# The delta rule's triangular inverses: substitution on VectorE in place of levels on TensorE

## The reference, cut to what matters

```python
def _delta_scan(q_c, k_c, v_c, kb_c, w_c):          # called for each of the two gates
    strict_lower = jnp.tril(jnp.ones((c, c), bool), -1)
    T0 = jnp.where(strict_lower, -(kb_c @ jnp.swapaxes(k_c, -1, -2)), 0.0)
    def inv_body(T, i):                              # row by row: T becomes the inverse, less I
        row = T[..., i, :]
        new = row + jnp.einsum('...k,...kc->...c', row, T)
        new = jnp.where(idx < i, new, row)
        return (T.at[..., i, :].set(new), None)
    T, _ = jax.lax.scan(inv_body, T0, jnp.arange(1, c))
    T = T + jnp.eye(c, dtype=T.dtype)
    u = T @ v_c                                      # kb_c = k * beta, v_c = v * beta
    wm = T @ kb_c
    def step(S, xs):                                 # then a scan over the 8 chunks
        q_i, k_i, u_i, w_i, wm_i = xs
        u_i = (u_i - wm_i @ S) * w_i[..., None]
        a = jnp.where(causal, q_i @ jnp.swapaxes(k_i, -1, -2), 0.0)
        return (S + jnp.swapaxes(k_i, -1, -2) @ u_i, q_i @ S + a @ u_i)
```

## Time and profile before

| | |
|---|---|
| median of 3 runs | 1379.96 us |
| span of the profiled execution | 1391.4 us, 11.4 us over that median |
| PE busy | 1265.5 us (91%), 18034 matmul records |
| DVE busy | 947.4 us (68%), 2038 instructions |
| ACT busy | 738.6 us (53%) |
| POOL busy | 679.6 us (49%) |

### The profile page before, as it was taken

How to read it: one execution, slowest core, us unless ns; L and a number is a source line. 1 busy time by engine, 2 the same in 40 slices (tenths; PEclk the granted TensorE clock), 3 DMA queues, 4 the chain that set the end, 5 groups by cost and what they waited for, 6 DMA issues and landing times.

```text
span 1391.4 us, 43177 instructions
## 1 busy us (share of the span) xinstructions
PE 1265.5 (91%) x18034; PEld 1007.5 (72%) x18034; DVE 947.4 (68%) x2038; ACT 738.6 (53%) x2084; POOL 679.6 (49%) x677
## 2 busy tenths in 40 slices
PE   5776869999999999899999899989999999889898
PEld 3444557777678788678887688767787778778776
DVE  3667688966777876677688668775758775475434
ACT  5577857654745663446765366435774355133221
POOL 3545346763473556256565355443736545304422
PEclk8899899999999999899999999999999999999999
DMA  5101056744366367265676357635565644647662
GB/s 198 59 11 62 1 196 191 228 123 149 114 206 210 128 196 247 95 203 181 215 229 192 104 191 231 206 134 172 168 200 166 206 167 160 221 147 233 189 226 99
DMA packets 90721, 231.44 MB, mean 166 GB/s; under 512 B 9376, under 2 KB 15648, under 8 KB 90400
## 3 DMA queue, kind: packets, MB, share of 16 engines
q1 hardware_dynamic: 90384, 228.09, 50.9%
q10 hardware_dynamic: 144, 0.59, 0.1%
HBM read 225.50 MB, written 3.15 MB: 164 GB/s over the span
## 4 chain that ended last, share of the span: by engine, by line
PE 71%; DVE 12%; issue 4%; ACT 3%; DMA 2%; POOL 1%; DVEq 0%; SPq 0%; ACTq 0%
PE bank L968 15%; PE bank L921 15%; PE bank L831 8%; PE bank L958 4%; PE bank L939 4%; PE bank L616 4%; PE bank L949 2%; PE bank L932 2%; PE bank L687 2%; PE bank L675 2%; DVE ogate L1405 2%; PE bank L711 2%; PE bank L651 1%; PE bank L721 1%; PE bank L661 1%
## 5 line engine op out<-in xcount | busy, mean ns | idle before, releaser
L1802 POOL TENSOR_TENSOR vgate<-vgate,xT 128x512 f32<-128x512 f32 x256 | 323.5, 1288 | 137.8 <-DMA vgate<-gates 137.6
L921 PE MATMUL bank<-wv,vgate 128*128 128x128 f32 x2048 | 258.7, 281 | 5.4 <-POOL vgate L1802 4.7
L921 PEld LDWEIGHTS bank<-wv,vgate 128*128 128x128 f32 x2048 | 247.3, 195 | 16.1 <-issue 11.0
L968 PE MATMUL bank<-ogate,wo 128*128 128x256 f32 x1024 | 251.4, 390 | 3.9 <-DVE ogate L1405 2.7
L968 PEld LDWEIGHTS bank<-ogate,wo 128*128 128x128 f32 x1024 | 191.7, 194 | 35.4 <-issue 10.2
L1405 DVE TENSOR_TENSOR ogate<-ogate,bank 128x1024 f32<-128x1024 f32 x128 | 153.4, 1211 | 37.1 <-PE bank L958 35.6
L1746 POOL TENSOR_TENSOR rot<-rot 128x512 f32<-128x512 f32 x64 | 81.9, 1280 | 108.4 <-DVE rot L1071 108.4
L1516 ACT ACTIVATE prob<-prob,mx 128x128 f32<-128x128 f32 (+1 forms) x256 | 96.0, 377 | 55.9 <-DVE mx L1095 55.6
L1758 POOL TENSOR_TENSOR prob<-prob,rsum 128x256 f32<-128x256 f32 (+1 forms) x64 | 60.1, 939 | 113.9 <-DVE rsum L1098 113.9
L1695 ACT ACTIVATE mprob<-bank,mmin 128x256 f32<-128x256 f32 x128 | 59.3, 469 | 100.7 <-DVE mmin L1394 100.4
L616 PE MATMUL bank<-wqkv,hT 128*128 128x512 f32 x192 | 103.9, 640 | 5.4 <-ACT hT L1452 4.7
(11 more groups left out here) (236 smaller groups left out, 2574.9 us busy)
## 6 DMA issues: line engine op xcount, KB each, us to landing
vgate<-gates SPq DMA_DIRECT2D x128, 512.0 KB, 4.5
ogate<-gates SPq DMA_DIRECT2D x128, 512.0 KB, 4.2
wv<-in_wv_moe SPq DMA_DIRECT2D x128, 256.0 KB, 4.9
wo<-in_wo_moe SPq DMA_DIRECT2D x128, 256.0 KB, 4.7
kv<-values SPq DMA_DIRECT2D x128, 128.0 KB
local<-in_local SPq DMA_DIRECT2D x1, 1715.0 KB, 10.5
wqkv<-in_wqkv SPq DMA_DIRECT2D x2, 768.0 KB, 7.0
x<-in_x SPq DMA_DIRECT2D x8, 128.0 KB, 8.5
```

The lines of the kernel that those rows point to most:

```text
L921: i = nc.tensor.matmul(out[:, n * D:(n + 1) * D], xg[:, e, n * P:(n + 1) * P], m.wv[slot][:, e, :], start=(q, n, e) == (0, 0, 0), stop=(q, ...
L968: i = nc.tensor.matmul(out[:, 0:T], m.wo[slot][:, e, :], cg[:, e, :], start=(h, q, e) == (0, 0, 0), stop=(h, q, e) == (MH - 1, 1, EQ - 1))
L1802: i = tt(gate[:, e:e + half, :], gate[:, e:e + half, :], spread(m.xT[b % 2][:, :], 1, half), ALU.mult)
```

## The change

The 64 systems of an image are solved by substitution on DVE instead of by levels on PE. POOL writes `lower`, the 16 unit lower triangles of each head, times beta, from `kmat` masked to the other side of the diagonal; `w0` has two instructions instead of four. `lanes`: one DVE transpose lays out each system on a partition of its own (4 heads x 2 x 16 systems = 128 partitions: each system twice, once for the even and once for the odd rows of the answer), in 32 rows of 32 columns, and a product with the constant `spot` makes the start of `solved` from beta. `sub`: for k = 31 down to 1, column k of the 16 rows, as far as they are not zero, times row k of the triangle is taken from the columns below k: a product into `step` and a subtraction in place, each of them reading two SBUF tensors. That is 62 instructions an image, each waiting for the one before it, in 8 parts of at most 4 values of k; other DVE work can stand between the parts. `dT` transposes `solved` into `winvT`. The four levels' `lev`, `levmul`, `levmask`, `levadd`, their transposes, `kT`, and ACT's `beta_col` are gone. All turn strings and the bank string are drawn anew, and `wo` on DVE has a wait more.

```diff
+SUBS = [range(k, max(k - 4, 0), -1) for k in range(CH - 1, 0, -4)]
 TENSOR_TURNS = (
-    "aaaaaaaaabbabaXGGGGbabbbaaabaabGaaabbbbbGcaabcbGbbbccbbGcGaabbabGaacaaacGGGbaGcbacbbcaaabbbGaabbGaaabbabbGbcab"
+    "GaaaaGGGaaaabbabXaabbbbabbabbGabacaaGaacabGcbacabGcGbbbaaabbGbaabbaaabbbGGGGcbacacbcGbbbcbbGbabaGbacaaGGcaaabc"
...
 def delta_ticks(b):
-    ticks = [[("kk", b)], [("dstart", b)], [("w0", b)], [], [], [], []]
-    for i in range(1, 5):
-        ticks += [[("lev", b, i)], [("levmask", b, i)], [("levmul", b, i, 0)], [("levmul", b, i, 1)], [("levadd", b, i)]]
-    ticks += [[("dT", b)], [], [], [("uw", b, 0)], [("uw", b, 1)], [("st0", b)]]
+    ticks = [[("kk", b)], [("dstart", b)], [("w0", b)], [("lanes", b)]] + [[("sub", b, part)] for part in range(len(SUBS))]
+    ticks += [[("dT", b)], [("uw", b, 0)], [("uw", b, 1)], [("st0", b)]]
...
-    def lev(b, i):
-        bank = banks.kept("masked", b, i)
-        out = split(take(bank)[:, 0:NC_ * CH], n=NC_)
-        pe.wait_ge(s.winvT, nth_winvT(b, i))
-        w4 = upper_columns(m.winv[:, :, :], i)
-        for c in range(NC_):
-            last = per_head(out[:, c, :].rearrange("p (a n t) -> p a n t", a=2, t=2 ** i), m.kT[:, c, :], w4[:, c::NC_, :, :], start=True, stop=True)
-        last.then_inc(bank.filled, 1)
-
-    def levmul(b, i, a):
...
-        for g in range(a * NC_, (a + 1) * NC_):
-            last = per_head(out[:, g, :], m.winvT[:, g, :], m.pmat[:, g, :], start=True, stop=True)
...
     def wo(b, l):
...
+        before = earlier(b, l, 1)
+        if before:
+            read = banks.of("w2", *before)
+            v.wait_ge(read.emptied, read.use)
...
-    def w0(b):
-        bank = banks.of("kk", b)
-        v.wait_ge(bank.emptied, bank.use)
-        v.chain(nc.vector.transpose(m.kT[:, :, :], m.kmat[:, :, :]))
-
-    def lev(b, i):
...
-        nc.vector.transpose(m.winvT[:, :, :], m.winv[:, :, :]).then_inc(s.winvT, 1)
-
-    def levmask(b, i):
...
-    def levadd(b, i):
...
+    def lanes(b):
+        v.wait_ge(s.w0, nth("w0", b))
+        v.chain(nc.vector.transpose(m.lanes[:, :, :], spread(m.lower[:, :, :], 2, 2)))
+        v.settle()
+        tt(m.solved[:, :, :], m.spot[:, :, :], spread(flat(m.lanes)[:, ::CH + 1], 1, CH // 2), ALU.mult).then_inc(s.lanes, 1)
+
+    def sub(b, part):
+
+        if part == 0:
+            v.wait_ge(s.lanes, nth("lanes", b))
+        for k in SUBS[part]:
+            rows = CH // 2 - k // 2
+            left, step = m.solved[:, k // 2:, 0:k], m.step[:, 0:rows * k].rearrange("p (j c) -> p j c", c=k)
+            v.settle()
+            v.chain(tt(step, spread(m.solved[:, k // 2:, k], 2, k), spread(m.lanes[:, k, 0:k], 1, rows), ALU.mult))
+            v.settle()
+            i = tt(left, left, step, ALU.subtract)
+            if k == 1:
+                i.then_inc(s.sub, 1)
+            else:
+                v.chain(i)
 
     def dT(b):
-        before = banks.kept("level", b, 4)
-        v.wait_ge(before.emptied, before.use)
-        nc.vector.transpose(m.winvT[:, :, :], m.winv[:, :, :]).then_inc(s.winvT, 1)
+        v.wait_ge(s.sub, nth("dT", b))
+        nc.vector.transpose(m.winvT[:, :, :].rearrange("p g i -> p i g"), flat(m.solved)).then_inc(s.winvT, 1)
...
-    def dgate(b, k):
...
-        act(m.beta_col[:, :, :], split(bank.ap, n=NG), ACT.Exp, scale=-1.0).then_inc(bank.emptied, 1)
...
-        a.chain(act(m.beta_col[:, :, :], m.beta_col[:, :, :], ACT.Ln, bias=one))
...
     def w0(b):
...
-        g.chain(tt(m.kmat2[:, :, :], m.kmat[:, :, :], spread(m.level_neg[:, 0:CH], 1, NC_), ALU.mult))
+        g.chain(tt(m.kmat2[:, :, :], m.kmat[:, :, :], spread(m.eye[:, :], 1, NC_), ALU.add))
         g.settle()
...
+        tt(m.lower.rearrange("p t (a c) -> p a c t", a=2), spread(m.kmat2[:, :, :], 1, 2), spread(m.gates[b % 2][:, 0:2, :], 3, CH),
+           ALU.mult).then_inc(s.w0, 1)
```

More of the change, by code:

```diff
@@ L54, in constants @@
     out["eye"] = r == c
-    out["below"] = c < r
+    out["above"] = c > r
     out["upper"] = c >= r
-    level = lambda s, c: (r // (2 * s) == c // (2 * s)) & (r // s % 2 == 1) & (c // s % 2 == 0)
-    upper = lambda s: c[:, c[0] // s % 2 == 0]
-    out["level_neg"] = -1.0 * np.concatenate([level(1, c)] + [level(s, upper(s)) for s in (2, 4, 8, 16)], axis=1)
+    spot = 2 * np.arange(CH // 2)[:, None] + np.arange(2)[:, None, None] == np.arange(CH)[None, :]
+    out["spot"] = np.repeat(spot, NG, axis=0)[np.arange(P) % (2 * NG)]
     out["first"] = np.broadcast_to(ME - np.arange(ME)[None, :], (P, ME))
@@ L158 @@
     "layer1": {"w_delta": (P, 3, D), "conv": (P, 3, CONV), "w_gate": (P, 4, P), "gate_b": (P, 2), "dnorm": (P, CH), "wo_delta": (P, D),
-               "headsum": (P, P), "eye": (P, CH), "below": (P, CH), "upper": (P, CH), "level_neg": (P, CH + 4 * CH // 2), "first": (P, ME),
+               "headsum": (P, P), "eye": (P, CH), "above": (P, CH), "upper": (P, CH), "spot": (P, CH // 2, CH), "first": (P, ME),
                "route": (P, 1), "sel": (P, P)},
@@ L329 @@
 KEPT = [("gla_sum", "gsum", (0,)), ("delta_sum", "dout", (0,)), ("moe_sum", "mproj", (0, 0)), ("values", "hv", (0,)),
-        ("scores", "mscore", ()), ("context", "mctx", ()), ("masked", "lev", ()), ("level", "levmul", (0,))]
+        ("scores", "mscore", ()), ("context", "mctx", ())]
 BANKS = {"xnT": 1, "proj": 1, "projv": 1, "qkT": 1, "lscore": 2, "probT": 1, "pv": 1, "wo": 1, "lnorm": 1,
@@ L334 @@
          "gsend": 1, "fuse": 2, "mqk": 1, "mpT": 1, "mend": 1}
-ON_TENSOR = [*BANKS, "gsum", "dout", "mproj", "hv", "mscore", "mctx", "lev", "levmul", "dwo"]
+ON_TENSOR = [*BANKS, "gsum", "dout", "mproj", "hv", "mscore", "mctx", "dwo"]
 class Banks:
@@ L864, in uw @@
         pe.wait_ge(s.vkc, nth("dstart", b))
[L865 removed]
+        pe.wait_ge(s.winvT, nth("dT", b))
         for c in range(NC_):
@@ L1300, in kk @@
         out = filled(bank).rearrange("p (c a t) -> p c a t", c=NC_, a=2)
-        v.chain(tt(m.kmat[:, :, :], out[:, :, 1, :], spread(m.below[:, :], 1, NC_), ALU.mult))
+        v.chain(tt(m.kmat[:, :, :], out[:, :, 1, :], spread(m.above[:, :], 1, NC_), ALU.mult))
         tt(m.do[:, :, :], out[:, :, 0, :], spread(m.upper[:, :], 1, NC_), ALU.mult).then_inc(bank.emptied, 1)
-    def w0(b):
-        bank = banks.of("kk", b)
-        v.wait_ge(bank.emptied, bank.use)
-        v.chain(nc.vector.transpose(m.kT[:, :, :], m.kmat[:, :, :]))
@@ L1324, in levadd @@
-    def levadd(b, i):
-        bank = banks.kept("level", b, i)
-        w = upper_columns(m.winv[:, :, :], i)
-        tt(w, w, filled(bank)[:, 0:NG * CH // 2].rearrange("p (g n t) -> p g n t", g=NG, t=2 ** i), ALU.add).then_inc(bank.emptied, 1)
+    def lanes(b):
[3 more added lines that the diff above has]
+        tt(m.solved[:, :, :], m.spot[:, :, :], spread(flat(m.lanes)[:, ::CH + 1], 1, CH // 2), ALU.mult).then_inc(s.lanes, 1)
```

165 lines of the change are left out of this document (63 added, 102 removed).

## The result

The changed kernel takes 1446.4 us (median of four runs, 1441.4 to 1450.6) against 1380.4 of the kernel before in the same session (1379.4 to 1390.6): 1.048 times as long, with a 95% interval of 1.043 to 1.054. It is slower, the forecast of 1328 us was wrong, and the time lies outside the range.

What follows compares the result with a forecast made beforehand. PE was taken as the bound behind 200 us. 1391.4 - 60.2 (levels' matmuls) - 29.6 (issue idle) + 30 (loss) = 1331.6 us profiled; 1328 was taken without profiler, range 1286 to 1404.

Steps and rivals of the forecast that it cites:

- the loss of PE: PE waiting for late DVE work, between `kk` and `uw` and before the MoE's matmuls: 30 us, bounds 0 and 90.
- the relief itself: Levels' small matmuls (60.2 us) and issue idle before them (29.6 us) leave PE: 89.8 us, all on the path.
- The waits put down to issue: PE idle in front of the levels' matmuls, out of tiny instructions, waiting for nobody: 29.6 us, all counted as gain.
- rival 3: Changed order loses elsewhere what PE gains, by banks, `wo`'s new wait, blocks of eight: 60 to 90 us; chance 0.14.
- the 11.4 us: Median of before lies 11.4 us below its profile; profiling may cost this in the dense bursts of tiny instructions.
- The records of PE: Sign on PE: matmul records fall by 6144 from 18034 to 11890.
- the substitution's plain duration: On DVE, 62 undisturbed two-source instructions an image, 5712 columns: 15.8 us an image.
- the price of the waits for POOL: Extra time of DVE's new two-source instructions while POOL works: 0.15 us each, 74 us in all.
- the list of signs: What the trace after would show, such as DVE busy near 1110 us and `uw` waiting for `dT` in images 2, 7.
- Rival 2: DVE becomes the bound through POOL in the substitution's blocks, 0.43 us extra each: some 1404 us without profiler; chance 0.21.
- Rival 1: All the new DVE work is covered by the order's slack, no loss on PE: 1291 to 1302 us; chance 0.19.
- Rival 4: PE's issue waits are made by profiling, so only 60.2 less 30 us is gained: 1350; within the forecast's 0.46.

Runs made afterwards that it cites:

- e6: e4 with the substitution cut to its last product and subtraction, inverses left out of the computation: 1321.6 us, 0.956 of before.
- e9: The changed kernel with the substitution cut to its last product and subtraction, inverses left out of the computation: 1357.7 us, 0.983 of before.
- e2: The changed kernel with each product and subtraction of the substitution replaced by a one-source sum over as many columns: 1379.5 us, 0.997 of before.
- e3: The kernel before with the levels' small matmuls for one chunk of eight, their results set to zero: 1326.3 us, 0.958 of before.
- e7: e4 with one-source sums in place of the substitution's products and subtractions: 1393.8 us, 1.008 of before.
- e10: The changed kernel, substitution whole, with POOL's 256 gate-by-activation products turned into one-source multiplications by a constant: 1386.1 us, 1.002 of before.
- e4: The changed kernel's whole substitution, computation complete, in the turns and banks of the kernel before: 1454.5 us, 1.051 of before.
- e8: e2 with only one sum in each pair instead of two, half of the plain load: 1356.0 us, 0.983 of before.

## Why the prediction was wrong

**The step that failed is the loss of PE, set at 30 us with 0 and 90 as its bounds** ("Is there room on DVE?"). On its own terms the sum had 1205.3 us of busy PE and 126.3 us of idle. The trace has 1220.0 and 224.2: 97.9 us more idle, 14.7 us more busy. Counted as the prediction counted, from 1391.4 - 89.8 = 1301.6 us without any loss, the loss was 142.6 us. The spans of e6, e9, e2 and after (1323.0, 1356.5, 1373.5, 1444.2) part it, in the order in which the pieces were put in:

- 21.4 us: the relief itself (e6). PE's busy time falls by 77.2 us, more than the 60.2 counted (the earlier trace rows itself has 47.0 + 25.0 = 72.0), but PE's idle time is 134.7 us, where it should have been 96.3. The waits put down to issue do go, from 35 to 3 us; in their place PE waits longer for DVE (33 to 53) and for ACT (21 to 38), 10.0 us of it for the inverses' last transpose, where it had been 1.4. The forecast took the issue waits as gain in full; e3 found the same, 58 us for 78.
- 33.5 us: the redrawn order with nothing to hide (e9 against e6). This is rival 3's loss, at half of its price and without its means, as e9 has no blocks of eight on DVE. The prediction put it at nothing.
- 17.0 us: the plain load of the substitution (e2 against e9), sums in place of products. It was the larger part of the load, 123.4 of 193.0 us, and costs least in this order; in the old one it is 68 of span (e7 against e6).
- 70.7 us: the waits for POOL (after against e2), 69.6 us long.

The span of before from which all this is counted, 1391.4 us, is a long one: most of its later timings lie from 1375 to 1390. By medians the four parts are 29, 36, 22 and 67 us, each to some 5 us, so only the first depends on it. The prediction's guess that profiling costs the 11.4 us is not borne out: the other spans lie within 6 us of their medians, on either side.

**Why 30 was believable and false.** I counted only what DVE had more than PE between `kk` and `uw` of an image. That takes for granted that within such a window of 30 to 60 us each engine can run ahead of the other as far as it likes. The order is fixed, and PE's next matmul hangs on a softmax or a gating that stands behind the next block of the substitution. Four instructions that take 4.8 us instead of less than 1 make somebody late. The sums over a window said "room" where the chain after says that the two engines take turns, and it is the waits for `ogate`, `vmoe` and `mprob` that grew (e9 against after). That what is lost there is never made up, because nothing of the order moves, is a reading that no run tests.

**The clock is part of the loss.** The same 11890 records make PE busy for 1188.3 us in e6 and for 1220.0 after, at granted clocks of 0.963 and 0.940; 1188.3 x 0.963 / 0.940 is 1217. Busy time times clock is 1135 to 1150 us in all nine kernels of the table with these records, so the longer busy time goes with the clock. On the whole the clock is lower where PE waited more (0.963 with 135 us idle, 0.940 with 224, 0.926 with 231), though not from row to row (0.945 and 0.947 with 182); that the waits lower it is argued from this, not tried. The prediction had no term for it.

**What was right.** The records of PE; the substitution's plain duration, 126 us forecast and 123.4 measured by e2; the price of the waits for POOL, 74 forecast and 69.6 measured, 0.14 us each, though the mean hides what it is made of (undisturbed instructions and some of 1.1 to 1.4 us); DVE's busy time, 1127 and 1122 (the list of signs has 1110 for it); the chain's DVE share above 12%. The price is in part luck: 0.15 us was taken between 0.05 and 0.43, below the 0.20 of its own working, with no row behind the choice. `uw` waits for `dT` in two images and for next to nothing, but in images 4 and 7, not 2 and 7. The waits for POOL were weighed and priced rightly, and then given to the order to absorb. The Trainium skill, "GPSIMD Engine Reference", section Key points, names the shared SBUF interfaces as a cause of contention. By that rule, the runs agree: e2 and e10 shorten the waits from either side.

**Slightly off.** `lanes` takes 1.24 + 1.41 us an image and not 1.29 + 0.70, `dT` 1.06 and not 0.70: 1.0 us an image. The product with `spot` (L1275) takes 1.10 us in the four images where it meets nothing of POOL's, so 0.4 us of its excess and the 0.36 of `dT` are left to the strided reads and writes that I had put at nothing, which no run varied apart; the other 0.3 us of its mean is waiting for POOL:

```profile
L1275 DVE TENSOR_TENSOR dlt<-layer,uw 128x512 f32<-128x512 f32 x8 | 11.3, 1410 | 0.3
L1273 DVE STREAM_TRANSPOSE uw<-winvT 128x1024 f32<-128x1024 f32 x8 | 9.9, 1236 | 1.5 <-POOL winvT L1729 1.4
L1295 DVE STREAM_TRANSPOSE winvT<-dlt 128x512 f32<-128x512 f32 x8 | 8.5, 1059 | 0.3 <-DVE ogate L1368 0.2
```

**The rivals.** Rival 2 had the right place, the waits for POOL in the blocks of the substitution, and the nearest time (1404), with a wrong price and a wrong point of decision: it wanted 0.38 us extra an instruction before the change would lose. The trace has 0.14 and the change loses by 66 us, because a load need not fill DVE to be on the path. By the prediction's own criterion (waits of PE behind 200 us above 90, DVE under 90%) rival 3 is the one met: 170 us at 80%. But e4 shows that the order as such is not the main cause. Rival 1, all covered, holds only for the first half of the plain load (e8), and its time, 1291 to 1302, is not reached even with no load at all (e6 1321.6, e9 1357.7). Rival 4 had the size of the relief: 60 us without the issue waits, and e6 gains 61, e3 58. Its reason, that profiling makes these waits, is not shown; what e6 shows is that other waits take their place.

**What stays open.** Why the load is free at first in the new order and then costs its length, 0 for 47 us of DVE (e9 to e8), 24 for the next 61 (to e2), 67 for the last 64 (to the change), isn't settled: that the order was laid out for about this plain load is argued from e7, where the old order pays 72 us for 104 from the start. Why the new order is slower than the old one when unloaded is seen in its chain (DMA 14%) and in POOL's waits for the gates of `vgate`, twice as long as in the old one, but wasn't tried apart. And no run has the whole computation and beats the kernel before: e4 and the change, the only two, lose.

## What to carry to other kernels

What was taken from the bound engine, matmuls and the idle time in front of them, came back as three quarters of its length here (58 us of 78), and the load put on the other engine cost anything from nothing to its full length, which it reached with that engine 77% busy: weigh a move by these two prices, not by the idle share of the engine that takes it. Count instructions with two SBUF sources on VectorE while GpSimd is at work at their waiting length (0.39 us for 0.25 here, with GpSimd busy for 46% of the time), and ask first whether a one-source form, on either engine, will do. When an order is redrawn for a change, time it without the change's load as well: here it lost 34 us that way, which only the pair e6 and e9 brought to light.

## What the hardware showed unexpectedly

- A two-source DVE instruction that meets a two-source POOL instruction of 1.29 us ends just behind it, 30 columns or 128 alike (1.15 to 1.24 us), and so one by one for each of POOL's. With one source on DVE's side (e2) the same place runs undisturbed:

```profile
272.51 1.27 POOL L1748 TENSOR_TENSOR vgate<-vgate,xT 128x512 f32<-128x512 f32 x1
272.73 0.28 DVE L1285 TENSOR_REDUCE step<-dlt 128x7 f32<-128x126 f32 x1
273.05 0.28 DVE L1287 TENSOR_REDUCE step<-dlt 128x7 f32<-128x126 f32 x1
273.36 0.29 DVE L1285 TENSOR_REDUCE step<-dlt 128x8 f32<-128x136 f32 x1
```

- With one source on POOL's side DVE is let through about 0.6 us after POOL's instruction starts, 0.9 us before its end, and almost always only the first DVE instruction that meets one of POOL's is held (e10: DVE's at 273.74 is 0.30 us longer than alone, the two behind it run at 0.30 and 0.29). The Trainium skill, "Trainium Architecture — The Big Picture", section What this means for kernel authors, calls the port pair that the two engines share an exclusive lock and no split of bandwidth. By that rule, the trace after agrees; in e10 DVE is held for less than POOL's instruction lasts.
- POOL's multiplication by a constant is slower than its product of two tensors, 1.51 against 1.30 us on 128x512.
- A product on 512 columns with one source read at a stride of 33 takes 1.10 us at least, where the 158 ns and 1.05 ns a column of the earlier trace rows give an estimate of 0.70, and a transpose of 512 columns whose output is scattered takes 1.06, against 0.71 for the plain one in the earlier trace rows.
